# An attention and feed-forward layer in fp32: where the last weights are split, in what order GpSimd takes its last tasks, and which buffer the second residual goes to

## What is computed

```
x = x + attn(layernorm(x), gamma, w_qkv, w_out)   # rms_norm, 16 heads of 64, softmax, no mask
x = x + ffn(layernorm(x), router_w, w1, b1, w2, b2)

def ffn(x):                                       # 4096 tokens
    p, _  = top_k(softmax(x @ router_w), 2)       # 8 experts, one shared set of weights
    p     = p / sum(p)
    return (gelu(x @ w1 + b1) @ w2 + b2) * sum(p) # w1: 256 x 1024, w2: 1024 x 256
```

## Time and profile before

| | us |
|---|---|
| median of three runs | 1227.94 |
| the three runs | 1227.82, 1227.94, 1230.18 |
| profiled execution, its own time | 1231.42 |
| its span in the profile | 1229.6 |
| TensorE busy in the span | 1192.9 |
| VectorE busy | 959.6 |
| ScalarE busy | 892.7 |
| GpSimd busy | 646.8 |
| TensorE's granted clock, mean | 0.996 |

### The profile page before, as it was taken

One profiled execution on the slowest core, in us unless ns is written; L12 is line 12 of the kernel. 1 busy time (PEld: TensorE's weight loads), 2 busy tenths in 40 slices (PEclk: granted clock), 3 DMA queues, 4 the chain that ended last, 5 costly groups with the idle time before them and its releaser, 6 DMA issues. The chain is left out here.

```text
span 1229.6 us, 29275 instructions
## 1 busy us (share of the span) xinstructions
PE 1192.9 (97%) x11355; PEld 1044.5 (85%) x11355; DVE 959.6 (78%) x1735; ACT 892.7 (73%) x1926; POOL 646.8 (53%) x801
## 2 busy tenths in 40 slices
PE   7999999999999999999999999999999988999998
PEld 5778888888888888888888888888888877888887
DVE  6788788878887888778878887888778855666644
ACT  5788888878887888788878888888787873344432
POOL 5565556555655565556555655565555674322221
PEclk9999999999999999999999999999999999999999
DMA  4122111311131113111311131113111232111100
GB/s 157 36 53 70 36 36 37 86 36 35 36 87 36 36 36 87 36 36 36 87 35 36 36 87 36 36 35 87 35 36 36 70 87 66 42 44 60 35 18 35
DMA packets 32633, 62.92 MB, mean 51 GB/s; under 512 B 5744, under 2 KB 9072, under 8 KB 32496
## 3 DMA queue, kind: packets, MB, share of 16 engines
q1 hardware_dynamic: 32496, 61.05, 19.3%
HBM read 19.08 MB, written 8.39 MB: 22 GB/s over the span
## 5 line engine op out<-in xcount | busy, mean ns | idle before, releaser
L826 POOL TENSOR_SCALAR prob<-prob,rowinv 128x512 f32<-128x512 f32 x512 | 348.7, 694 | 312.2 <-DVE rowinv L998 309.6
L743 ACT ACTIVATE prob<-ps,negmax 128x512 f32<-128x512 f32 x512 | 346.5, 685 | 36.0 <-DVE negmax L993 32.0
L925 DVE TENSOR_TENSOR pT_lo<-ps,pT_hi 128x512 fp32r<-128x512 f32 (+1 forms) x384 | 320.4, 862 | 28.0 <-ACT pT_hi L734 21.5
L993 DVE TENSOR_REDUCE negmax<-ps 128x2 f32<-128x1024 f32 x256 | 311.1, 1216 | 1.1 <-PE ps L472 1.1
L496 PEld LDWEIGHTS ps<-identity,prob 64*128 64x128 f32 x4096 | 153.9, 139 | 74.4 <-issue 35.6
L731 ACT ACTIVATE pT_hi<-ps 128x1024 fp32r<-128x1024 f32 x128 | 131.4, 1026 | 106.0 <-issue 103.3
L496 PE MATMUL ps<-identity,prob 64*128 64x64 f32 x4096 | 177.6, 226 | 15.9 <-POOL prob L826 9.6
L468 PE MATMUL ps<-nat 64*128 64x512 f32 x1024 | 171.5, 411 | 1.4 <-DVE nat L925 1.4
L510 PE MATMUL ps<-pT_hi,vbuf 128*128 128x256 f32 x1024 | 164.8, 283 | 3.0 <-DVE pT_lo L925 3.0
L510 PE MATMUL ps<-pT_lo,vbuf 128*128 128x256 f32 x1024 | 164.5, 283 | 0.0
L510 PEld LDWEIGHTS ps<-pT_hi,vbuf 128*128 128x128 f32 x1024 | 144.6, 190 | 10.0 <-DVE pT_lo L925 4.2
(11 more groups left out here) (115 smaller groups left out, 2291.5 us busy)
## 6 DMA issues: line engine op xcount, KB each, us to landing
att_hi_v<-halves_out SPq DMA_DIRECT2D x128, 128.0 KB, 2.3
att_lo_v<-halves_out SPq DMA_DIRECT2D x128, 128.0 KB, 2.4
xres<-in_x SPq DMA_DIRECT2D x8, 512.0 KB, 3.5
x_scratch<-xres SPq DMA_DIRECT2D x8, 512.0 KB, 2.8
out_y<-f_o SPq DMA_DIRECT2D x16, 256.0 KB, 2.2
xin<-in_x SPq DMA_DIRECT2D x7, 512.0 KB, 3.8
wstage<-in_w SPq DMA_DIRECT2D x4, 512.0 KB, 4.3
xin<-x_scratch SPq DMA_DIRECT2D x3, 512.0 KB, 3.7
```

The costliest lines, as they stand in the source:

```text
L743: act.activation(prob[:, n % NPROB, j * SEQ:(j + 1) * SEQ], ps[:, PS_SCORE[n % 2] + j, :], ACT.Exp, bias=negmax[:, n % 4, j:j + 1], accum_ ...
L826: return pool.tensor_scalar(dst, src, scalar, 1.0, ALU.mult, ALU.mult)
L925: return dve.tensor_tensor(dst, full, hi, ALU.subtract)
L993: dve.tensor_reduce(negmax[:, n % 4, :], ps[:, PS_SCORE[n % 2]:PS_SCORE[n % 2] + 2, :], AX.X, ALU.max, negate=True).then_inc(s_max, 1)
```

## The change

It has three parts, all at the hand-over.

1. Chunks 8 to 11 leave `POOL_CHUNKS`, so their lo parts are made on VectorE, in the same slots, and chunk 10 is split in slot 256 instead of slot 254. Its load is issued as before; chunk 11's load follows in slot 257.
2. On GpSimd, `attention_out(63)`, the last pair, stands behind `hidden_hi(2)` and `hidden_hi(3)` instead of ahead of them, and `powers(9)` stands ahead of `hidden_hi(2)` instead of behind `hidden_hi(4)`.
3. The second x1 goes to slice 2 of `prob` (unit 254's) instead of slice 0 (unit 255's); the third gelu buffer takes slice 0 in exchange. SyncE loads it in slot 257, once unit 254 is transposed, ahead of chunk 11 and of the last `regroup`. Its statistics stand on VectorE in slot 258 ahead of `hidden_lo(0)`; its normalisation stands behind `hidden_lo(3)`.

The order of TensorE's instructions is the same as before.

```diff
-        f_x1 = [xin[:, :, :], prob[:, 0, :].rearrange("p (t d) -> p t d", t=TT), xres[:, :, :]]
+        f_x1 = [xin[:, :, :], prob[:, 2, :].rearrange("p (t d) -> p t d", t=TT), xres[:, :, :]]
-        f_h = [prob[:, 1, 0:SEQ], prob[:, 1, SEQ:2 * SEQ], prob[:, 2, 0:SEQ]]
+        f_h = [prob[:, 1, 0:SEQ], prob[:, 1, SEQ:2 * SEQ], prob[:, 0, 0:SEQ]]
...
-        POOL_CHUNKS = (0, 2, 3, 4, 5, 6, 7, 8, 9, 10, 11)
+        POOL_CHUNKS = (0, 2, 3, 4, 5, 6, 7)
-        slot_of_chunks.update({NUNIT - 6: [8], NUNIT - 4: [9], NUNIT - 2: [10], NUNIT + 2: [11]})
+        slot_of_chunks.update({NUNIT - 6: [8], NUNIT - 4: [9], NUNIT: [10], NUNIT + 2: [11]})
...
+                if slot == UP_SLOT + 1:
+                    sp.wait_ge(s_pt, 2 * NUNIT - 2)
+                    load_x1(1)
...
-            sp.wait_ge(s_pt, 2 * NUNIT)
-            load_x1(1)
...
-            attention_out(NPAIR - 1)
             for c in range(B):
                 for f in range(len(HIDDEN_SLOTS) if c == 0 else 0, FT):
+                    if c == 0 and f == len(HIDDEN_SLOTS):
+                        powers(B + 1)
+                    if c == 0 and f == TT:
+                        attention_out(NPAIR - 1)
                     hidden_hi(c * FT + f)
-                    if c == 0 and f == TT:
-                        powers(B + 1)
...
+                if slot in HIDDEN_SLOTS:
+                    if slot == HIDDEN_SLOTS[0]:
+                        for t in range(TT):
+                            ffn_stats(1, t)
+                    hidden_lo(HIDDEN_SLOTS.index(slot))
...
                     hidden_lo(c * FT + f)
-                    if c == 0 and f in (2, 3):
-                        for t in (0, 1):
-                            ffn_stats(1, 2 * (f - 2) + t)
-                    if c == 0 and f == 4:
+                    if c == 0 and f == TT - 1:
+                        ffn_normalise(1)
                         routing_shift(0)
                 if c == 0:
-                    ffn_normalise(1)
```

More of the change, by code:

```diff
@@ L392, in regroup, with load_x1 @@
                 sp.dma_start(att_lo_v[DH:P, :], src[0:DH, 1, :]).then_inc(s_merge, 16)
+            def load_x1(c):
+                sp.dma_start(f_x1[c % 3], x1_dram[c]).then_inc(s_fx1[c % 3], 16)
             for slot in range(FIRST_SLOT, LAST_SLOT + 1):
                 b, rel = divmod(slot, SPB)
+                if slot == UP_SLOT + 1:
+                    sp.wait_ge(s_pt, 2 * NUNIT - 2)
+                    load_x1(1)
                 if rel == 24 and b + 2 < B:
@@ L419, in _ @@
                         load_weight(sp, i + 1)
-            def load_x1(c):
-                sp.dma_start(f_x1[c % 3], x1_dram[c]).then_inc(s_fx1[c % 3], 16)
             def store_out(c, part):
@@ L1007, in slot_tasks @@
                     lo(first_parts[1], first_stage, first_parts[0]).then_inc(s_first_lo, 1)
-                if slot in HIDDEN_SLOTS:
-                    hidden_lo(HIDDEN_SLOTS.index(slot))
                 for i in weight_slots(slot):
```

## The result

The changed kernel takes **1220.08 us** (median of four runs, 1219.72 to 1220.44); the kernel before took 1227.88 on the same chip (four runs, 1225.88 to 1230.18). The ratio is 0.992, with a 95% interval of 0.9901 to 0.9939. The forecast was 1219.2, in a range of 1217.6 to 1222.8.

The account below looks back on a forecast made before the run. TensorE, busy 1192.9 of 1229.6 us, was taken as the bound, leaving only waits and low clock to win. Gains 2.07 + 1.50 + 3.50 + 1.71 = 8.8 us off the 1227.94 median gave 1219.2, range 1217.6 to 1222.8.

Parts of the forecast that it names:

- (a): Up to transpose 254: with chunk 10 later, ScalarE copies the halves without waiting for its load; gain 2.07 us.
- (b): Transpose 254 to 255: 5.56 us by ScalarE's chain instead of 7.06; gain 1.50 us if the clock stays up.
- (c): Transpose 255 to `up(0, 7)`: `hidden_lo(2)` done 1.0 us ahead of need, whole wait gone; gain 3.50 us.
- (d): Last pair, `up(0, 7)` to `down(0, 0)`: pair fits with 0.7 us to spare, low clock gone; gain 1.71 us.
- step (e): Chunks 8 and 9 on VectorE: cost taken as 0 to 0.3 us; GpSimd's 2.4 us back each useless.
- rival 1: Clock falls anyway behind the first wait's remaining 0.8 us: 7.3 us gained, 1220.6, or 1222.4; chance 0.17.
- The contention that the prediction weighed: VectorE instructions with two SBUF inputs contend with GpSimd for shared SBUF interfaces: slowed between 1.6 and 2.5 times.
- the bound of 3.42: Upper price in us of VectorE's 1024-column weight subtraction, scaled from the 2.99 us row of 896 columns beside GpSimd.
- The walk along the last pair: `regroup(63)` at 1016.0, halves at GpSimd 1021.9, `attention_out(63)` done 1025.2, needed by the last outs at 1025.9.
- 2, the new order is late: ScalarE, GpSimd and the last pair wait too long, delaying `up(0, 7)` or last outs: 1219.9 to 1221.9; chance 0.13.
- 3, VectorE as the bound: All lo parts on VectorE at 3.42 us: gain only 4.3 us, 1223.6; chance 0.07.
- 4, slower: Load 11 so late that GpSimd holds everything: at 12 us of lateness slower by 2.5, 1230.4; chance 0.03.

Follow-up runs that it names:

- before_again: The kernel before, unchanged, run and profiled once more: 1227.97 us, ratio 1.0004.
- e_pool_subtracts: The changed kernel with all four weight subtractions on GpSimd again, chunk 10 still in slot 256: 1227.04 us, ratio 0.997 to the kernel before.
- e1_chunk10_back: The changed kernel with chunk 10 in slot 254 again, VectorE still subtracting: 1221.91 us, ratio 0.9944 to the kernel before.
- before_warm: The kernel before with 12 matmuls whose result nothing reads, ahead of TensorE's wait at `up(0, 7)`: 1228.80 us, ratio 1.0007.
- p13_pair_ahead: The changed kernel with the last pair ahead of `hidden_hi(2)` again, behind `powers(9)`: 1228.96 us, ratio 0.9978 to the kernel before.
- p1_weights_only: The kernel before with part 1 only (chunks 8 to 11 subtracted on VectorE, chunk 10 in slot 256): 1226.87 us, ratio 0.9976.
- part 2 alone: The kernel before with only the last pair moved behind `hidden_hi(2)` and `(3)`; `powers(9)`, second x1 and weights stay: 1229.22 us, ratio 0.9986.
- add_first: The changed kernel with VectorE's addition to `xres` ahead of the inverse of unit 255 in step 128: 1219.61 us, ratio 0.9938 to the kernel before.

## Why the prediction was right, and where it was not

Forecast times are turned into distances from transpose 254 (forecast at 1004.50).

| step | forecast | measured |
|---|---|---|
| (a) transpose 254 sooner | 2.07 | 2.06 |
| (b) transposes 254 to 255 | 5.56, gain 1.50 | 5.54, gain 1.52 |
| (c) 254 to `up(0, 7)` | 18.9, no wait | 18.84, no wait |
| (d) `up(0, 7)` to `down(0, 0)` | 8.3 | 7.94 |
| sum | 8.8 | 9.19 (8.66 against before_again) |

**(a), right.** The later slot gives the 2.07 us by itself, as forecast (2.06 in e_pool_subtracts). What I didn't see is that VectorE's subtracting gives 1.55 of them as well, so that the two edits overlap here. That is a sentence in step (e) that failed: "GpSimd gets 2.4 us back each, of use to no one". The use was not GpSimd's free time, but the earlier end of a subtraction that lets the next load go. I had read the row that begins at that very end, and did not ask what a faster engine would trigger. For chunk 11 step (c) walks through VectorE's subtraction, and there e_pool_subtracts shows its worth: 3.25 us.

**(b), right in size, with the wrong one of two bounds.** I took the later of TensorE's own work at the full clock (5.39) and ScalarE's chain over the table load (5.56). In the changed kernel the chain ends at 1006.98 + 0.59 = 1007.57, 5.27 us behind transpose 254, and transpose 255 starts at 5.54:

```profile
1004.03 1.05 ACT L770 ACTIVATE wbig_hi<-wstage 128x1024 fp32r<-128x1024 f32 x1
1005.10 1.28 ACT L761 ACT_TABLE_LOAD   x1
1006.39 0.69 ACT L761 ACTIVATE prob<-ps,b_sb 128x512 f32<-128x512 f32 x1
1006.98 0.59 ACT L754 ACTIVATE halves_out<-ps 128x512 f32<-128x512 f32 x1
```

e1_chunk10_back, without the hi part of chunk 10 in this chain, has 5.53, and so has before_warm, the code of before at the full clock: TensorE's own work is the bound, and my 5.39 for it, worked out from a mean clock, was 0.14 short.

before_warm also shows that the 1.5 us weren't there to win in every execution of the kernel before. The prediction said so under rival 1, as a condition; of four traces with those waits, three fell to the low clock and one didn't. In that one, 0.84 of the 1.51 us were still there at `up(0, 7)` and at `down(0, 0)`. That is a part of the way from 9.19 us in one pair of traces to 7.8 in the medians. The rest isn't settled.

**(c), right, with more slack than forecast.** The forecast left 1.0 us at `hidden_lo(2)`; p13_pair_ahead shows some 1.7. The term that was mis-sized is the subtraction of a weight chunk on VectorE, taken at 2.0 and bounded by 1.39 and 3.42. All four took 1.21 to 1.23 us, below the lower bound, and the two on the critical chain were among them. (1.39 was twice a row of 512 columns, so what an instruction costs whatever its length is in it twice.) VectorE and GpSimd beside each other in the changed kernel:

```profile
1005.37 1.21 DVE L927 TENSOR_TENSOR wbig_lo<-wstage,wbig_hi 128x1024 fp32r<-128x1024 f32 x1
```

```profile
1004.17 1.30 POOL L847 TENSOR_TENSOR att_hi_v<-att_hi_v,att_lo_v 128x512 f32<-128x512 f32 x1 [0.85 <-DMA att_lo_v<-halves_out]
1005.56 1.51 POOL L827 TENSOR_SCALAR attT_hi<-att_hi_v 128x512 fp32r<-128x512 f32 x1
```

The contention that the prediction weighed is there, but the other engine paid. VectorE started at 1005.37, GpSimd's rounding 0.19 us later, and it took 1.51 us; in e1_chunk10_back, where nothing ran beside it, 0.62. It ended 0.49 us after VectorE had. The normalisation of 4.08 us is the same the other way round: it starts 0.33 us behind GpSimd's addition and is slow as long as the pair lasts:

```profile
1017.47 1.69 DVE L927 TENSOR_TENSOR pT_lo<-prob,pT_hi 128x512 fp32r<-128x512 f32 x2 [1.20 <-POOL pT_hi L836]
...
1018.76 1.55 POOL L847 TENSOR_TENSOR att_hi_v<-att_hi_v,att_lo_v 128x512 f32<-128x512 f32 x1 [0.73 <-DMA att_lo_v<-halves_out]
1020.40 0.62 POOL L827 TENSOR_SCALAR attT_hi<-att_hi_v 128x512 fp32r<-128x512 f32 x1
1021.11 1.29 POOL L853 TENSOR_TENSOR attT_lo<-att_hi_v,attT_hi 128x512 fp32r<-128x512 f32 x1
```

And the 2.99 us of the earlier trace rows started behind a GpSimd subtraction already under way. They ended 0.96 us behind its end (13.64), so their excess was what was left of GpSimd's instruction; scaling them by the columns, as the bound of 3.42 does, had no ground. The Trainium skill states this ("SBUF — State Buffer", Who interferes with whom): the pair of ports that the two share is an exclusive lock, and issue order decides who is blocked. The trace agrees here: 1.21 us for the one that was first, and 1.51 instead of 0.62 for the other. I had used the rule that they contend, and not the one that says who pays.

Where the two start within some 0.03 us of each other, the start in the trace doesn't tell who pays. Beside chunk 9's subtraction (993.19, 1.23 us, at its free price) GpSimd's row starts 0.03 us sooner, and it is GpSimd that is slow, 3.74 us for four multiplications of which two alone take 1.36:

```profile
993.16 3.74 POOL L827 TENSOR_SCALAR prob<-prob,rowinv 128x512 f32<-128x512 f32 x4 [0.26 <-DVE rowinv L1000]
```

Step (e) put chunks 8 and 9 at nothing for VectorE, and so it was. This microsecond on GpSimd was not in it, and it cost nothing either: the distance ahead is 18.66 us, as with GpSimd's own subtractions (e_pool_subtracts).

**The walk along the last pair** was close. It forecast `attention_out(63)` 17.4 us after transpose 254 and its end at 20.7, ahead of a need at 21.4; it started at 16.5 and was done at 20.1 (1018.76, and 1021.11 + 1.29). From the first DMA of `regroup(63)` (1013.43) to the addition it took 5.33 us instead of 5.85, in spite of SyncE's third issue taking 1.68 us (1.86 before), where the `regroup(62)` that the 5.85 come from had 0.60; the pair itself took 3.64 instead of 3.30.

**(d), right in size (7.94 for 8.3), half wrong in its cause.** The step says that 1.71 us of 9.89 "are low clock", as if the clock alone were in the way. before_warm takes the low clock away and gets nothing: the tokens of batch 1 are as late. Part 3 alone doesn't get it either. p13_pair_ahead has early tokens and the low clock, and the stretch takes 9.37 us; p1_weights_only, with late tokens and the low clock, has 9.88. So the early tokens alone are worth 0.51, and the other 1.43 come only when the clock stays up as well. The two delays lie over each other, and the stretch falls to 7.94 only where both are gone: part 3 takes away the late tokens, and part 2 the low clock, by the wait at `up(0, 7)` that it removes. The sign of the late tokens stood in the earlier trace rows: `powers(9)` at 1032.45, behind a wait for VectorE's statistics, with the normalisation still to come before TensorE's transposes at 1039.36. I divided the stretch by its clock instead of walking it, and so gave the x1 load a cost (nothing) and no gain. That the sum came out right here is in part luck: the change happened to remove both.

**The rivals.** 1, the clock falls anyway: it did not, in any of the eight traces that have the 0.86 or 0.87 us that were left. 2, the new order is late: it was early. But p13_pair_ahead shows its place: with the pair ahead, the same waits cost 5.05 us. 3, VectorE as the bound: excluded by the 1.21 to 1.23 us. 4, slower: nothing near it.

**The parts.** I added up the terms as if they were independent. That was safe for the whole change and would have been wrong for any piece: for part 2 alone by the terms (c) and (d) one would forecast 5.2 us, and its distances gained 2.15, 1.5 of which went in the tail.

## What to carry to other kernels

Where stretches of waiting follow one another, price a change by walking each chain to the next place where TensorE asks for something, and then ask what is late there: removing one wait of 3.5 us brought out one of 2.9 at the next place, and taking away a low clock in the shadow of a late operand brings nothing until the operand comes sooner too. When work moves from one engine to another, follow who waits for its end (here a load through a single buffer), and not only the time that the engine gets back. For two engines that contend, take from the trace which of them starts clearly first: in the pairs here it kept its price, and the other one paid.

## What the runs showed of the hardware that I had not expected

- VectorE's subtraction of 1024 columns from two SBUF inputs took 1.21 to 1.23 us, also with GpSimd reading beside it, where VectorE had started 0.19 us sooner, and where GpSimd had by 0.03. GpSimd's rounding behind it went from 0.62 to 1.51 us. VectorE's normalisation, four instructions that read one tensor each, went from 1.37 to 4.08 us beside GpSimd's addition, rounding and subtraction.
- The granted clock fell to half (0.57 to 0.67 over 4.0 to 4.5 us) behind waits of 3.50, 3.46, 3.23, 3.05 and 2.93 us. It did not fall behind waits of 2.33, 2.00, 1.23 and 0.87. Behind the pair of waits of 1.64 to 1.74 and 1.12 us it fell in three traces of four. The same waits are thus no certain cause.
- One of SyncE's four issues of the last `regroup`, mostly the third, took 1.23 to 2.17 us in each of the fourteen traces (1.86 before, 1.68 in the changed kernel), where the issues around it took 0.46 to 0.62. The four of `regroup(62)` took 0.47 to 0.61. No run tells why.
- The times of one kernel lie up to 6.7 us apart (before_again, 1225.58 to 1232.32), while the distances from the fixed block on agree to 0.1 us in the changed kernel. The 0.55 us of add_first could only be seen in the distances.
